# A two-layer graph network on one core: y and the norm's numbers get a place per graph, the weights land in other tiles and in another order

## The chip, the cores and the metric

The kernel runs on one core of a Trainium2 chip. The metric is the device time of one execution in microseconds. TensorE (PE) multiplies, VectorE (DVE), ScalarE (ACT) and GpSimd (POOL) do the element-wise work, and SyncE (SP) issues every DMA. Each engine works through its own queue in order and waits at semaphores for the others.

## The reference

128 graphs of 128 nodes with 384 features pass two attention layers with 12 heads of 32, each with a residual and a layer norm:

```python
# layer 0
q, k, v = x @ Wq.T, x @ Wk.T, x @ Wv.T + bv
scores = q @ k.T * 384**-0.5 + (adj + adj)      # per head
p = softmax(scores)                              # rows of zeros give 0
x = layernorm(x + (p @ v) @ Wo.T + bo)
# layer 1
q, k, v = x @ Wq + bq, x @ Wk + bk, x @ Wv + bv
scores = where(adj > 0, q @ k.T / sqrt(32) + beta * adj, -9e15)
x = layernorm(x + softmax(scores) @ v)
```

## The kernel before

The graphs go in 64 pairs (graph 0 and 1 of a pair). The projections of layer 0 and 1 and the output product of layer 0 take three TensorE products for each one of float32: a tile is split into a high part (ACT) and a low part (DVE or POOL), and hi·hi, hi·lo and lo·hi are added (`split_product`, L371 to L373). So each of the seven weight matrices is loaded once into a staging place (`w_stage`), copied to `w_hi` by ACT (L511) and `w_lo` is subtracted by DVE (L658) or POOL (L849).

A software pipeline written out by hand sets the order. Each engine has a `body(r, off)` that names its steps for pair n and for pairs up to four back (m1 to m4) or one ahead (p1). Bodies for n = -1 to 6 stand unrolled, then a loop of two bodies a turn runs 28 times, and eleven more bodies drain the pipeline. A helper does nothing where its pair does not exist. The queues of the engines are in that written order, so a step that waits holds everything behind it on its engine.

A graph of layer 0 passes: `scores` (PE, L421), `negate` (DVE, L699: negated scores and row minimum), `exps` (ACT, L594), `fold_scores0` (POOL, L901 and L904), `abs_max` and `inverse_sums0` (DVE), `normalise0` (POOL, L919), `flip_probs` (DVE, L715: 32x32 transposes into the tile `flip0`), `spread_probs` (SP, four DMAs from `flip0` to `prob0T`), `attend` (PE, L437), `project_out0`, `add_residual0` (DVE, L667), `norm_stats_of` (DVE), `inverse_std` (POOL, L859 to L866) and `norm_apply0` (ACT, L573). Layer 1 ends with `attention_out1` (DVE, L765), `residual1` (POOL, L911), the same norm steps, `norm_apply1` (ACT, L579) and `store` (SP, L265). `flip0` is also the scratch of `fold_scores0`, which therefore waits until the DMAs out of it have landed.

There is one tile `y[layer]` and one set of `stats`, `mean_var`, `var_eps`, `rstd` and `shift` for each layer. So `add_residual0` of a graph waits for `norm_apply0` of the graph before (`x1_done`), and `attention_out1` waits for the store of the graph before (`stored`).

Staging places are tiles that are otherwise used later: WV0 and WQ0 lie in `stage`, WK0 in `neg_s1`, WO0 in `prob1`, WQ1 in `prob1T`, WK1 in `prob0T`, WV1 in `prob0`. In the body of the first pair (`is_peeled`) the first writer of each such tile waits for the `w_lo` of the matrix in it: `exps` of layer 0 for WV1, `spread_probs` of layer 0 for WK1. POOL makes the low parts of WO0, WQ1, WK1 and WV1 at the end of its body -1, ahead of its body 0.

Four PSUM banks (`r_bank`) serve as a ring for the tiles in `RING_USERS`, each in the bank of its index modulo 4; the other four hold scores.

Of the kernel before, what the change touches and what calls it, by code (L numbers as in the profile page):

```python
# [53 lines left out]
RING_USERS = ["pv0_0", "ot_0", "g1_0", "v0_1", "g1_1", "v1_0", "g1_2", "pv1_1",  # L54
              "xt0", "wo_0", "v1_1", "xt1", "ot_1", "pv0_1", "g1_3", "g0_0",
              "g1_4", "g0_1", "g0_2", "wo_1", "g0_3", "g0_4", "g1_5", "g0_5",
              "pv1_0", "x1t0", "x1t1", "v0_0"]
# [54 lines left out]
def build(nc, x, adj, wts, bv0, bo0, bq1, bk1, bv1, beta, out):  # L112

    with ExitStack() as ctx:
# [9 lines left out]
        def sems(name, n=2):  # L124
# [30 lines left out]
        neg_max = [sb(f"neg_max{l}", [P, H]) for l in range(2)]  # L155
        prob = [sb(f"prob{l}", [P, H, N]) for l in range(2)]
        row_sum = [sb(f"row_sum{l}", [P, H]) for l in range(2)]
        inv_sum0 = sb("inv_sum0", [P, H])
        inv_sum1 = [sb(f"inv_sum1_{g}", [P, H]) for g in range(2)]
        inv_raw0 = sb("inv_raw0", [P, H])  # L160
        sum_neg0 = sb("sum_neg0", [P, H])
        abs_max0 = sb("abs_max0", [P, H])
# [5 lines left out]
        flat = [stage[:, 0:C * D], stage[:, C * D:NS * C * D]] + [t.rearrange("p a b -> p (a b)")[:, 0:C * D] for t in (  # L168
            neg_s[1][:], prob[1][:], probT[1][:].rearrange("p i h b -> p i (h b)"),
            probT[0][:].rearrange("p i h b -> p i (h b)"), prob[0][:])]  # L170
# [3 lines left out]
        y = [sb(f"y{l}", [P, D]) for l in range(2)]  # L174
        stats = [sb(f"stats{l}", [P, 6]) for l in range(2)]
        mean_var = [sb(f"mean_var{l}", [P, 2]) for l in range(2)]
        var_eps = [sb(f"var_eps{l}", [P, 1]) for l in range(2)]
        rstd = [sb(f"rstd{l}", [P, 1]) for l in range(2)]
        shift = [sb(f"shift{l}", [P, 1]) for l in range(2)]
# [14 lines left out]
        stored = sem("stored")  # L194
        w_hi_done = sem("w_hi_done")
# [40 lines left out]
        def _(sp):  # L236
# [25 lines left out]
            def store(q, g):  # L262
                if q.valid():
                    sp.wait_ge(x2_done, q.count(1, g, 1))
                    sp.dma_start(out[bass.ds(2 * q.index() + g, 1)].rearrange("g (j a) d -> a j (g d)", j=NB), y[1][:]  # L265
                                 ).then_inc(stored, 16)
# [61 lines left out]
            sp.wait_ge(stored, 16 * NG)  # L328
# [3 lines left out]
        def _(pe):  # L332
# [174 lines left out]
        def _(act):  # L507
            def high_weights(*which):
                for i in which:
                    act.wait_ge(w_loaded[i], 16)  # L510
                    act.activation(w_hi[i][:], w_stage[i], ACT.Copy).then_inc(w_hi_done, 1)  # L511
# [56 lines left out]
            def norm_apply0(q, g):  # L568
                if q.valid():
# [29 lines left out]
            def body(r, off):  # L599
# [17 lines left out]
                high_xT(p1, 1)  # L617
                exps(1, m3, 1, 0, 2)
# [357 lines left out]
```

## Time and profile before

| | us |
|---|---|
| median of 3 runs (2166.12 to 2169.29) | 2168.59 |
| the profiled execution | 2169.0 |
| its span, first to last instruction | 2167.2 |
| PE busy in it | 2072.6 |

All of the numbers below are of that one profiled execution; 1.8 us of its time lie outside the span. The page's slices show the fill (some 100 us) and the drain (some 130 us) with PE partly idle, and between them 9 tenths or more in every slice. A busy PE means that matmuls were in flight; their ends are modelled.

### The profile page before, as it was taken

To read this page: it belongs to the slowest core of one execution; us is meant where nothing else is said; L and a number is where in the kernel's file an instruction comes from. 1 tells how busy PE (TensorE), PEld (TensorE's weight loads), DVE (VectorE), ACT (ScalarE), POOL (GpSimd) and SP (SyncE) were. 2 spreads that over 40 slices of the span, in tenths; PEclk is the share of its full clock that TensorE was granted. 3 is DMA by queue.
4 is the path that set the end of the run, shared out by engine and by line. 5 is a ranking of instruction groups with operands and counts; after the bars stand their busy time and mean duration, and the time that the engine had idled before them with its cause. 6 is when DMAs were issued, how large, how long until landed. Compare 5 with 4: busy or idle time off the path is not lost.

```text
span 2167.2 us, 86729 instructions
## 1 busy us (share of the span) xinstructions
PE 2072.6 (96%) x23808; PEld 1911.8 (88%) x23808; DVE 1858.4 (86%) x8451; ACT 1835.6 (85%) x7688; POOL 1517.4 (70%) x2060
## 2 busy tenths in 40 slices
PE   5899999999999999999999999999999999999974
PEld 4799999999999999999999999999999999999963
DVE  2588898998898898898898898899899899889874
ACT  4489889888888888888988888988888988888874
POOL 3567777777777777777777777777777777777752
PEclk8899999999999999999999999999999999999986
DMA  4255565555565555565555556556556556555544
GB/s 127 62 132 143 136 155 145 135 152 138 137 153 137 137 153 139 134 153 141 139 146 149 132 145 151 136 140 154 135 139 152 144 136 152 139 137 151 132 120 107
DMA packets 234778, 300.33 MB, mean 139 GB/s; under 512 B 26704, under 2 KB 226384, under 8 KB 234576
## 3 DMA queue, kind: packets, MB, share of 16 engines
q1 hardware_dynamic: 234576, 298.43, 55.0%
q14 instruction: 172, 1.41, 0.2%
q8 instruction: 30, 0.49, 0.1%
HBM read 46.67 MB, written 25.17 MB: 33 GB/s over the span
## 4 chain that ended last, share of the span: by engine, by line
PE 73%; DVE 11%; issue 9%; POOL 3%; DMA 1%; DVEq 1%; SPq 1%; ACT 1%; POOLq 0%; ACTq 0%
PE r_bank L371 18%; PE r_bank L373 17%; PE r_bank L372 17%; PE s_bank L421 9%; PE r_bank L437 7%; DVE neg_s L699 5%; PE r_bank L354 2%; PE r_bank L449 2%; DVE x1T_lo L721 1%; DMA prob0T<-flip 1%; DVE neg_max L699 1%; DVE flip L715 1%; PE r_bank L364 1%; DVE v L776 1%; DVE sum_neg L748 1%
## 5 line engine op out<-in xcount | busy, mean ns | idle before, releaser
L594 ACT ACTIVATE prob<-neg_s,neg_max 128x128 f32<-128x128 f32 x3072 | 1190.4, 394 | 97.8 <-DVE flip L715 81.2
L594 ACT ACTIVATION_READ_ACCUMULATOR prob<-neg_s,neg_max 128x1 f32 x3072 | 593.1, 193 | 0.0
L919 POOL TENSOR_TENSOR prob<-prob,inv_sum 128x512 f32<-128x512 f32 x384 | 388.9, 1041 | 257.3 <-DVE inv_sum L787 257.3
L699 DVE CUSTOM_DVE_ANT_0 neg_s<-s_bank,bias 128x128 f32<-128x128 f32 x1536 | 334.7, 285 | 67.3 <-PE s_bank L421 63.7
L371 PE MATMUL r_bank<-xT_hi,w_hi 128*128 128x256 f32 x1152 | 329.2, 286 | 20.8 <-DVE xT_lo L721 19.3
L371 PE MATMUL r_bank<-x1T_hi,w_hi 128*128 128x256 f32 x1152 | 338.2, 294 | 6.7 <-DVE x1T_lo L721 3.3
L699 DVE CUSTOM_DVE_ANT_0 neg_s<-s_bank,adj 128x128 f32<-128x128 f32 x1536 | 333.4, 285 | 3.4 <-issue 2.8
L373 PE MATMUL r_bank<-xT_hi,w_lo 128*128 128x256 f32 x1152 | 328.0, 285 | 0.0
L372 PE MATMUL r_bank<-xT_lo,w_hi 128*128 128x256 f32 x1152 | 327.9, 285 | 0.0
L373 PE MATMUL r_bank<-x1T_hi,w_lo 128*128 128x256 f32 x1152 | 326.3, 283 | 0.0
L372 PE MATMUL r_bank<-x1T_lo,w_hi 128*128 128x256 f32 x1152 | 325.6, 283 | 0.0
L901 POOL TENSOR_TENSOR flip<-neg_s 128x768 f32<-128x768 f32 x128 | 234.6, 1832 | 102.2 <-DMA prob0T<-flip 100.0
L699 DVE DVE_READ_ACCUMULATOR2_ANT neg_max<- 128x1 f32 x3072 | 254.7, 83 | 0.0
L371 PEld LDWEIGHTS r_bank<-xT_hi,w_hi 128*128 128x128 f32 x1152 | 220.8, 192 | 22.6 <-DVE xT_lo L721 19.8
L371 PEld LDWEIGHTS r_bank<-x1T_hi,w_hi 128*128 128x128 f32 x1152 | 218.2, 189 | 25.5 <-issue 12.6
L715 DVE STREAM_TRANSPOSE flip<-prob 128x1536 f32<-128x1536 f32 x128 | 227.3, 1776 | 10.6 <-POOL prob L919 2.6
L715 DVE STREAM_TRANSPOSE stage<-prob 128x1536 f32<-128x1536 f32 x128 | 226.8, 1772 | 1.8 <-DMA prob1T<-stage 1.8
L373 PEld LDWEIGHTS r_bank<-xT_hi,w_lo 128*128 128x128 f32 x1152 | 221.0, 192 | 0.0
L372 PEld LDWEIGHTS r_bank<-xT_lo,w_hi 128*128 128x128 f32 x1152 | 220.8, 192 | 0.0
L372 PEld LDWEIGHTS r_bank<-x1T_lo,w_hi 128*128 128x128 f32 x1152 | 218.9, 190 | 0.0
L373 PEld LDWEIGHTS r_bank<-x1T_hi,w_lo 128*128 128x128 f32 x1152 | 218.6, 190 | 0.0
L776 DVE TENSOR_TENSOR v<-r_bank,bv_row 128x384 f32<-128x384 f32 x256 | 139.4, 545 | 45.1 <-issue 34.2
(82 smaller groups left out, 5332.0 us busy)
## 6 DMA issues: line engine op xcount, KB each, us to landing
prob0T<-flip SPq DMA_DIRECT2D x512, 192.0 KB, 3.5
prob1T<-stage SPq DMA_DIRECT2D x512, 192.0 KB, 3.6
x_in<-in_x_dram SPq DMA_DIRECT2D x128, 192.0 KB, 3.6
x_late<-x SPq DMA_DIRECT2D x64, 384.0 KB, 4.2
out_dram<-y SPq DMA_DIRECT2D x128, 192.0 KB, 2.4
adj<-in_adj_dram SPq DMA_DIRECT2D x256, 64.0 KB, 2.4
stage<-in_L_gnn_Wv_dram SPq DMA_DIRECT2D x1, 576.0 KB, 5.8
stage<-in_L_gnn_Wq_dram SPq DMA_DIRECT2D x1, 576.0 KB, 6.7
```

The costliest lines, as they stand in the source:

```text
L354: mm = pe.transpose(ring(f"xt{g}")[:, c * P:(c + 1) * P], x_in[q.parity][:, g, c * P:(c + 1) * P], ident[:])
L371: pe.matmul(dst, a_hi(c), b_hi(c), start=(c == 0), stop=False)
L372: pe.matmul(dst, a_hi(c), b_lo(c), start=False, stop=False)
L373: mm = pe.matmul(dst, a_lo(c), b_hi(c), start=False, stop=(c == C - 1))
L421: mm = pe.matmul(s_bank[j][:, c * N:(c + 1) * N], qT[layer][q.parity][rows, c, m], kT[layer][q.parity][rows, c, m], start=True, stop=True)
L437: mm = pe.matmul(ring(name)[HD * j:HD * (j + 1), c * N:(c + 1) * N], v[layer][q.parity][:, g, f], probT[layer][:, :, HC * c + j, :], start ...
L594: act.activation(prob[layer][:, h, :], neg_s[layer][:, h, :], ACT.Exp, bias=neg_max[layer][:, h:h + 1], scale=-1.0, accum_out=row_sum[laye ...
L699: dve.tensor_tensor_reduce(neg_s[layer][:, h, :], s_bank[b][:, (h // HC) * N:(h // HC + 1) * N], (adj0, bias1)[layer][q.parity][:, g, :], ...
L715: dve.transpose(flip[layer].rearrange("p (j h b) -> p h j b", j=NB, h=H), prob[layer][:].rearrange("p h (j a) -> p h j a", j=NB)).then_inc ...
L776: dve.tensor_tensor(v[layer][q.parity][:, g, :], ring(f"v{layer}_{g}")[:, 0:D], bv_row[layer][:], ALU.add).then_inc(v_out[layer], 1)
L901: pool.tensor_tensor(fold_a, neg_s[0][:, :, 0:N // 2], neg_s[0][:, :, N // 2:N], ALU.add).then_inc(fold_steps, 1)
L919: pool.tensor_tensor(prob[0][:, hs, :], prob[0][:, hs, :], inv_sum0[:, hs].unsqueeze(2).to_broadcast([P, HC, N]), ALU.mult).then_inc(probn ...
```

## The change

1. `y` and the norm's numbers exist for each layer and graph of a pair. The waits for the previous graph become waits for the same graph of the previous pair; `stored` is split in two semaphores.
2. The weights are loaded in the order WQ0, WK0, WV0, WO0, WQ1, WK1, WV1 and lie in: WV0 and WO0 in `stage`, WQ0 in `prob0`, WK0 in `prob0T`, WQ1 in `neg_s1`, WK1 in `prob1`, WV1 in `prob1T`. The waits for `w_lo` at the first pair name these. `w_hi_done` becomes one semaphore for each matrix.
3. WO0 is split in the middle of body -1, its low part by DVE instead of POOL. POOL makes the low parts of WQ1, WK1 and WV1 at the end of body 0.
4. `project_v` waits for the low part of its input (`lo_done`), which it did not before.
5. `RING_USERS` is rotated by nine places; as 28 is a multiple of 4, that renames the banks (each index one lower, modulo 4) and leaves which tiles share one.
6. Ten small tiles of 12 columns become slices of one tile `heads`. With it the start of `prob0`, `prob1`, `flip0`, `prob0T` and `prob1T` in SBUF moves from byte 128 of a 256-byte block to byte 224; the tiles `y` start at byte 224 too.

```diff
-RING_USERS = ["pv0_0", "ot_0", "g1_0", "v0_1", "g1_1", "v1_0", "g1_2", "pv1_1",
+RING_USERS = ["wo_0", "v1_1", "xt1", "ot_1", "pv0_1", "g1_3", "g0_0", "g1_4",
...
+        flat = [stage[:, 0:C * D], prob[0], probT_rows[0], stage[:, C * D:NS * C * D], neg_s[1], prob[1], probT_rows[1]]
...
+        y = [[sb(f"y{l}_{g}", [P, D]) for g in range(2)] for l in range(2)]
+        norm = [[sb(f"norm{l}_{g}", [P, 11]) for g in range(2)] for l in range(2)]
...
             load_x(Pair(0, 0))
-            load_weights(WV0)
             load_weights(WQ0)
+            load_weights(WK0)
             for layer, b_ in enumerate((bv0, bv1)):
                 sp.dma_start(bv_row[layer][:], b_.partition_broadcast(P)).then_inc(bv_loaded, 16)
-            load_weights(WK0)
+            load_weights(WV0)
...
-                        sp.wait_ge(w_lo_done[(WK1, WQ1)[layer]], 1)
+                        sp.wait_ge(w_lo_done[(WK0, WV1)[layer]], 1)
...
                     read[BANK[name]] = (v_out[layer], q.off, 1, g, 1)
+                    pe.wait_ge(lo_done[layer], q.count(1, g, 1))
...
-                            act.wait_ge(w_lo_done[(WV1, WO0)[layer]], 1)
+                            act.wait_ge(w_lo_done[(WQ0, WK1)[layer]], 1)
...
                 high_xT(p1, 1)
+                if is_peeled(r, off, -1):
+                    high_weights(WO0)
...
                 if is_peeled(r, off, -1):
-                    high_weights(WO0, WQ1, WK1, WV1)
-
-            high_weights(WV0, WQ0, WK0)
+                    high_weights(WQ1, WK1, WV1)
+
+            high_weights(WQ0, WK0, WV0)
...
-                    dve.wait_ge(x1_done, q.count(1, g, 0))
-                    dve.tensor_tensor(y[0][:], ring(f"wo_{g}")[:, 0:D], x_bo[q.parity][:, g, :], ALU.add
+                    dve.wait_ge(x1_done, q.plus(-1).count(1, g, 1))
+                    dve.tensor_tensor(y[0][g][:], ring(f"wo_{g}")[:, 0:D], x_bo[q.parity][:, g, :], ALU.add
...
-                    dve.wait_ge(stored, q.count(16, g, 0))
+                    dve.wait_ge(stored[g], q.plus(-1).count(8, 1, 8))
...
                 low_xT(p1, 1)
+                if is_peeled(r, off, -1):
+                    low_weights(WO0)
...
                 fold_scores0(n, 1)
-                if is_peeled(r, off, -1):
-                    low_weights(WO0, WQ1, WK1, WV1)
+                if is_peeled(r, off, 0):
+                    low_weights(WQ1, WK1, WV1)
```

POOL's queue from its first wait on, before; `w_lo3` to `w_lo6` are the low parts of WO0, WQ1, WK1 and WV1, `flip0` rows are `fold_scores0`, `prob0` rows `normalise0`:

```order
L849 TENSOR_TENSOR w_lo3<-prob1,w_hi3 128x1152
L849 TENSOR_TENSOR w_lo4<-prob1T,w_hi4 128x1152
L849 TENSOR_TENSOR w_lo5<-prob0T,w_hi5 128x1152
L849 TENSOR_TENSOR w_lo6<-prob0,w_hi6 128x1152
L901 TENSOR_TENSOR flip0<-neg_s0 128x768
L904 TENSOR_TENSOR flip0<-flip0 128x384
L919 TENSOR_TENSOR prob0<-prob0,inv_sum0 128x512 x3
L878 TENSOR_TENSOR x_bo0<-x_in0,bo_row 128x384 x2
L901 TENSOR_TENSOR flip0<-neg_s0 128x768
L904 TENSOR_TENSOR flip0<-flip0 128x384
L919 TENSOR_TENSOR prob0<-prob0,inv_sum0 128x512 x3
```

And after:

```order
L901 TENSOR_TENSOR flip0<-neg_s0 128x768
L904 TENSOR_TENSOR flip0<-flip0 128x384
L919 TENSOR_TENSOR prob0<-prob0,heads 128x512 x3
L878 TENSOR_TENSOR x_bo0<-x_in0,bo_row 128x384 x2
L901 TENSOR_TENSOR flip0<-neg_s0 128x768
L904 TENSOR_TENSOR flip0<-flip0 128x384
L849 TENSOR_TENSOR w_lo4<-neg_s1,w_hi4 128x1152
L849 TENSOR_TENSOR w_lo5<-prob1,w_hi5 128x1152
L849 TENSOR_TENSOR w_lo6<-prob1T,w_hi6 128x1152
L919 TENSOR_TENSOR prob0<-prob0,heads 128x512 x3
```

One of the four subtractions has left the queue; the other three stand between the fold and the normalisation of graph 1 of the first pair.

ACT's queue from its start, before (`w_hi` rows are the weights, `xT_hi` the first pair's input, `prob` rows its first `exps`):

```order
L511 ACTIVATE w_hi<-stage 128x1152 x2
L511 ACTIVATE w_hi<-neg_s 128x1152
L519 ACTIVATE xT_hi<-r_bank 128x3x128 x2
L554 ACTIVATE q0T<-r_bank 128x256 x3
L554 ACTIVATE k0T<-r_bank 128x256 x3
L511 ACTIVATE w_hi<-prob 128x1152
L511 ACTIVATE w_hi<-prob1T 128x1152
L511 ACTIVATE w_hi<-prob0T 128x1152
L511 ACTIVATE w_hi<-prob 128x1152
L594 ACTIVATE prob,row_sum<-neg_s,neg_max 128x128 x8
```

And after:

```order
L507 ACTIVATE w_hi<-prob 128x1152
L507 ACTIVATE w_hi<-prob0T 128x1152
L507 ACTIVATE w_hi<-stage 128x1152
L515 ACTIVATE xT_hi<-r_bank 128x3x128 x2
L507 ACTIVATE w_hi<-stage 128x1152
L550 ACTIVATE q0T<-r_bank 128x256 x3
L550 ACTIVATE k0T<-r_bank 128x256 x3
L507 ACTIVATE w_hi<-neg_s 128x1152
L507 ACTIVATE w_hi<-prob 128x1152
L507 ACTIVATE w_hi<-prob1T 128x1152
L590 ACTIVATE prob,heads<-neg_s,heads 128x128 x8
```

WO0 has moved ahead of the first q and k evictions; three matrices are left in front of the first `exps`.

## Rows read from the trace of the kernel before

**Rows 1.** The page: span, busy time of each engine.

```profile
span 2167.2 us, 86729 instructions
PE 2072.6 (96%) x23808; PEld 1911.8 (88%) x23808; DVE 1858.4 (86%) x8451; ACT 1835.6 (85%) x7688; POOL 1517.4 (70%) x2060
```

**Rows 2.** Windows: stretch, its length, busy (instructions) by engine, PE clock, DMA.

```profile
200.00:2000.00 1800.00, 1786.15 (x20744) 1651.13 (x20743) 1615.35 (x7362) 1588.72 (x6688) 1312.63 (x1788) 1.00 0.57 143
```

**Rows 3.** Waits within 200 to 2000: us in total, times, longest.

```profile
PE r_bank L437 <- DVE v L776: 9.2, 27, 0.4
PE r_bank L371 <- DVE x1T_lo L721: 3.3, 11, 0.4
...
DVE neg_s L699 <- PE s_bank L421: 53.8, 56, 1.7
...
DVE y L667 <- ACT x L573: 24.9, 55, 0.5
```

**Rows 4.** Timeline of the fill: start, duration, instruction [idle before <-releaser].

```profile
7.25 0.44 SPq L278 DMA_DIRECT2D prob<-in_L_gnn_Wo_dram  x1
...
16.01 0.55 PE L371 MATMUL r_bank<-xT_hi,w_hi 128*128 128x256 f32 x1 [9.94 <-DVE xT_lo L721]
...
26.33 2.67 POOL L849 TENSOR_TENSOR w_lo<-prob,w_hi 128x1152 fp32r<-128x1152 f32 x1 [9.31 <-ACT w_hi L511]
...
28.29 0.29 DVE L699 CUSTOM_DVE_ANT_0 neg_s<-s_bank,adj 128x128 f32<-128x128 f32 x1 [0.53 <-PE s_bank L421]
...
36.69 1.80 POOL L901 TENSOR_TENSOR flip<-neg_s 128x768 f32<-128x768 f32 x1
...
36.76 0.40 ACT L594 ACTIVATE prob<-neg_s,neg_max 128x128 f32<-128x128 f32 x1 [7.35 <-POOL w_lo L849]
...
42.20 0.55 PE L371 MATMUL r_bank<-xT_hi,w_hi 128*128 128x256 f32 x1 [9.34 <-DVE xT_lo L721]
...
54.37 1.82 POOL L901 TENSOR_TENSOR flip<-neg_s 128x768 f32<-128x768 f32 x1 [6.17 <-DMA prob0T<-flip]
...
56.27 1.01 POOL L904 TENSOR_TENSOR flip<-flip 128x384 f32<-128x384 f32 x1
...
58.59 3.04 POOL L919 TENSOR_TENSOR prob<-prob,inv_sum 128x512 f32<-128x512 f32 x3 [1.31 <-DVE inv_sum L787]
...
63.48 0.40 ACT L594 ACTIVATE prob<-neg_s,neg_max 128x128 f32<-128x128 f32 x1 [6.75 <-DVE flip L715]
```

**Rows 5.** DMA issues: tile, size, median us from issue to landing.

```profile
prob<-in_L_gnn_Wo_dram SPq DMA_DIRECT2D x1, 576.0 KB, 7.9
...
prob0T<-flip SPq DMA_DIRECT2D x512, 192.0 KB, 3.5
```

**Rows 6.** Timeline of PE in the steady part.

```profile
1035.66 0.28 PE L373 MATMUL r_bank<-x1T_hi,w_lo 128*128 128x256 f32 x1
1035.78 0.28 PE L371 MATMUL r_bank<-xT_hi,w_hi 128*128 128x256 f32 x1
...
1058.37 0.28 PE L373 MATMUL r_bank<-x1T_hi,w_lo 128*128 128x256 f32 x1
1058.57 0.64 PE L437 MATMUL r_bank<-prob1T,v 128*32 128x128 f32 x16
```

**Rows 7.** Timeline of the drain.

```profile
2103.87 0.56 DVE L667 TENSOR_TENSOR y<-r_bank,x_bo 128x384 f32<-128x384 f32 x1 [2.33 <-ACT x L573]
...
2104.02 0.39 ACT L594 ACTIVATE prob<-neg_s,neg_max 128x128 f32<-128x128 f32 x1
...
2105.28 0.52 DVE L677 BATCH_NORM_STATS2 stats<-y 128x6 f32<-128x384 f32 x1
...
2106.34 0.21 POOL L859 TENSOR_SCALAR var_eps<-mean_var 128x1 f32<-128x1 f32 x1 [3.48 <-DVE mean_var L680]
...
2110.57 3.00 SPq L306 DMA_DIRECT2D prob1T<-stage  x4
...
2151.76 0.56 DVE L765 TENSOR_TENSOR y<-r_bank,inv_sum 128x384 f32<-128x384 f32 x1 [1.12 <-DMA out_dram<-y]
```

More of the change, by code:

```diff
@@ L154, in build @@
         neg_s = [sb(f"neg_s{l}", [P, H, N]) for l in range(2)]
-        neg_max = [sb(f"neg_max{l}", [P, H]) for l in range(2)]
+        heads = sb("heads", [P, 10 * H])
+        per_head = [heads[:, i * H:(i + 1) * H] for i in range(10)]
+        neg_max, row_sum, inv_sum1 = per_head[0:2], per_head[2:4], per_head[4:6]
+        inv_sum0, inv_raw0, sum_neg0, abs_max0 = per_head[6:10]
         prob = [sb(f"prob{l}", [P, H, N]) for l in range(2)]
[L157 to L162, printed above, removed]
         flip0 = sb("flip0", [P, H * N])
@@ L167, in build @@
         probT = [sb(f"prob{l}T", [P, NB, H, HD]) for l in range(2)]
-        flat = [stage[:, 0:C * D], stage[:, C * D:NS * C * D]] + [t.rearrange("p a b -> p (a b)")[:, 0:C * D] for t in (
-            neg_s[1][:], prob[1][:], probT[1][:].rearrange("p i h b -> p i (h b)"),
-            probT[0][:].rearrange("p i h b -> p i (h b)"), prob[0][:])]
+        probT_rows = [t[:].rearrange("p i h b -> p i (h b)") for t in probT]
+        flat = [stage[:, 0:C * D], prob[0], probT_rows[0], stage[:, C * D:NS * C * D], neg_s[1], prob[1], probT_rows[1]]
+        flat = [t if i in (WV0, WO0) else t[:].rearrange("p a b -> p (a b)")[:, 0:C * D] for i, t in enumerate(flat)]
         w_stage = [t.rearrange("p (c o) -> p c o", c=C) for t in flat]
@@ L173, in build @@
         o1T = sb("o1T", [P, C, N])
[L174 to L179, printed above, removed]
+        y = [[sb(f"y{l}_{g}", [P, D]) for g in range(2)] for l in range(2)]
+        norm = [[sb(f"norm{l}_{g}", [P, 11]) for g in range(2)] for l in range(2)]
+        stats, mean_var, var_eps, rstd, shift = ([[t[:, a:b] for t in n] for n in norm] for a, b in ((0, 6), (6, 8), (8, 9), (9, 10), (10, 11)))
         mask1 = sb("mask1", [P, N])
@@ L264, in store @@
                     sp.wait_ge(x2_done, q.count(1, g, 1))
[L265 to L266 removed]
+                    sp.dma_start(out[bass.ds(2 * q.index() + g, 1)].rearrange("g (j a) d -> a j (g d)", j=NB), y[1][g][:]
+                                 ).then_inc(stored[g], 16)
             def keep_x1(q):
@@ L326, in _ @@
             iterations(sp, body)
-            sp.wait_ge(stored, 16 * NG)
+            for g in range(2):
+                sp.wait_ge(stored[g], 8 * NG)
         @block.tensor
@@ L510, in high_weights @@
                     act.wait_ge(w_loaded[i], 16)
-                    act.activation(w_hi[i][:], w_stage[i], ACT.Copy).then_inc(w_hi_done, 1)
+                    act.activation(w_hi[i][:], w_stage[i], ACT.Copy).then_inc(w_hi_done[i], 1)
             def high_xT(q, g):
@@ L578, in norm_apply1 @@
                     act.wait_ge(rstd_steps[1], q.count(3, g, 3))
-                    act.activation(y[1][:], y[1][:], ACT.Identity, bias=shift[1][:], scale=rstd[1][:]
+                    act.activation(y[1][g][:], y[1][g][:], ACT.Identity, bias=shift[1][g][:], scale=rstd[1][g][:]
                                    ).then_inc(x2_done, 1)
@@ L692, in negate @@
                                 if is_peeled(q.r, q.off, 0):
-                                    dve.wait_ge(w_lo_done[WK0], 1)
+                                    dve.wait_ge(w_lo_done[WQ1], 1)
                                 dve.wait_ge(bias1_steps, q.count(3, g, 3))
@@ L712, in flip_probs @@
                             dve.wait_ge(w_lo_done[WV0], 1)
-                            dve.wait_ge(w_lo_done[WQ0], 1)
+                            dve.wait_ge(w_lo_done[WO0], 1)
                     dve.wait_ge(probT_loaded[layer], q.count(16 * NB, g, 0))
@@ L830, in body @@
                 low_x1T(m1, 0)
-            low_weights(WV0, WQ0, WK0)
+            low_weights(WQ0, WK0, WV0)
             iterations(dve, body)
```

38 lines of the change are left out of this document (19 added, 19 removed).

## The prediction

> **What bounds the kernel now.** I read the page first, then the windows by stage, then the waits of the steady part, and last the timelines of the fill and the drain. The page says that PE is busy for 2072.6 of 2167.2 us [rows 1], so some 95 us without PE are all that better covered waits could win. The window from 200 to 2000 shows where they are not: PE is idle there for 1800 - 1786.15 = 13.9 us in all, at the full clock [rows 2]. So about 81 of the 95 us lie in the fill and the drain, and each part of the change has to be read there apart from the 56 steady pairs.
>
> In the steady part the waits of PE itself come to 9.2 + 3.3 = 12.5 us [rows 3], all for DVE: 27 times (once a loop turn) for the tile v, 11 times for the low part of x1. The wait that the change takes away is another: DVE waits 55 times for ACT's norm result before it writes y, 24.9 us in all, or 0.45 us a pair. The reader is to see what comes after it on DVE: the layer-1 scores, for which DVE waits 56 times, 53.8 us in all, 0.96 us a pair [rows 3].
>
> In the fill the timeline tells a clear story [rows 4]. DVE has the first negated scores from 28.3 us on, but ACT's first exponential starts at 36.76 after 7.35 us of waiting for POOL's low weights: its output tile still holds WV1. POOL makes four of these from 26.33 to 36.69, 2.59 us each, and only then folds. PE stands for 9.34 us until 42.20 because of that. From there the chain goes round: fold, normalise, flip, DMA out of the flip tile, next fold. The second fold at 54.37 waited for the DMA, its second half starts at 56.27 and ends at 57.28, and graph 1 is normalised from 58.59; ACT had waited 6.75 us for the flip that follows.
>
> **The change part by part.**
>
> *The first exponentials.* After the change they wait for WQ0's low part, made before PE's first projection at 16.01. ACT then has three `w_hi` left in front of them instead of four and would be done by about 28.3; the first row minimum is there at about 28.6. I take 28.7 for the first exponential: 36.76 - 28.7 = 8.0 us earlier. POOL's first fold needs all twelve heads, which DVE gives 0.21 us apart, so it starts near 31.1 instead of 36.69 and ends near 34.0; the sums need the last exponential, 8.0 us earlier than before, at about 34.1. So the fold is no bound, and normalise, flip, DMA and the next fold all move by 8.0 us: that fold starts at 54.37 - 8.0 = 46.4 and ends at 49.3.
>
> *The subtractions are still to be done.* Three of them now stand behind this fold: 3 x 2.59 = 7.8 us, to 57.05. Graph 1's normalisation is behind them in POOL's queue and could have started at 58.59 - 8.0 = 50.6. It starts at 57.05. Of the 8.0 us there remain 58.59 - 57.05 = 1.5 us. Behind it wait DVE's flip, the exponentials of the next pair (the row at 63.48), through them the split of the input of the pair after, and PE. PE's gap of 9.34 us before 42.20 goes, and nearly as long a one comes back ten to twenty microseconds later. The chain of folds and DMAs then repeats as before, 1.5 us earlier, until PE is the bound from about 90 us on. I take -1.5 us. The bounds: 0 if the shorter gap at 42 and the longer one behind it leave PE at its lower clock for longer, and -8.0 if the three subtractions were hidden.
>
> *WO0 and the order of loads.* WQ0 and WK0 come first and WV0 third; but PE's first projection waits for the split of x, and that stands behind all three on ACT and on DVE, so 16.01 stays. WO0 is issued at 7.25 and lands 7.9 us later [rows 4, 5], at 15.2; ACT and DVE split it in a good microsecond each, ACT before PE has finished the first group of nine products begun at 16.01, DVE in a gap that lasts until the first v. Cost nothing; if WO0 landed two microseconds later, ACT would hold the first q by about one, which the same chain would carry: bound +1.
>
> *A place for each graph in the steady part.* DVE's wait of 0.45 us goes, all it does until the layer-1 scores comes 0.45 us earlier, and there it waits 0.96 + 0.45 us. Those scores are PE's, and PE waits for nothing that this stretch of DVE makes: its 12.5 us hang on work behind the scores, in the start of the next body. The norm's result gets earlier too, but ACT's queue is not what PE waits for. I take 0, with -12.5 us as the far end if all of PE's waits went.
>
> *The extra wait in `project_v`.* Four groups a pair, 256 in all, carry one more semaphore that has always been reached. What it costs PE is bounded by two group starts [rows 6]: a q or k group, which has two such waits, starts 0.12 us after the product before it, the same step as inside a group (1035.66 to 1035.78), so a second wait is hidden behind a 256-column product. An `attend` group with three waits starts 0.20 us after (1058.37 to 1058.57), 0.08 more. `project_v` will have two, thus nearer to the first: 0. The far end is 256 x 0.08 = 20 us.
>
> *The drain.* DVE's write of y of the last graph of layer 0 waits 2.33 us for ACT [rows 7]; that goes. Behind it stand the statistics of layer 1, the sum of the last exponentials (ended at 2104.02 + 0.39 = 2104.4) and then the statistics at 2105.28, which can now start 0.2 us after the sum, at 2104.6. POOL had idled 3.48 us for them, and behind it are ACT's norm, a store and the DMAs at 2110.57, which the rest of the drain needs. So -0.7 us. The wait of 1.12 us for a store before the write at 2151.76 goes too, but the other graph's flip, DMA and product end later than that branch: 0. The bounds are 0 and -2.3.
>
> *Banks and slices.* The rotation gives each tile the same neighbours in the ring, and slices of one tile need no more instructions: 0.
>
> The DMAs between `flip0` and `prob0T` take 3.5 us from issue to landing [rows 5], with rows of 1536 bytes that start at byte 128 of a 256-byte block, and will start at byte 224. The Trainium skill (DMA: Bandwidth & Descriptors, How a descriptor splits into AXI transactions) states that a first transaction that starts inside such a block still costs the beats from the block's start. By it a row goes from 52 to 55 beats of 32 bytes, so a transfer would take at most 6% longer, 0.2 us, which an estimate from that page would put on some six transfers of the fill and drain: +1.2 us. No row here shows two alignments of one transfer, so the sum leaves it out.
>
> *The sum.* -1.5 - 0.7 = -2.2 us on an execution of 2169.0 us gives 2166.8. The median of the runs is 0.4 us below that execution, so I predict 2166.5 us.
>
> **The rivals.** What this kernel's measurement can tell from no change is about 0.2%, 4.3 us.
>
> *A, the forecast*: 2166.5, the fill's gain is handed back at the three subtractions. Its own range is 2164.3 to 2169.5.
>
> *B, the fill's gain stays.* If POOL's subtractions were covered, 8.0 + 0.7 us would go: 2159.9. For it speaks that POOL idles 6.17 us before the fold at 54.37; against it, that this idle time is ahead of the fold and the subtractions are behind it in an ordered queue. 7%.
>
> *C, the steady part follows.* DVE's 0.45 us reach PE, and the 12.5 us of PE's waits go: 2168.6 - 2.2 - 12.5 = 2154; a third of it would already be told from no change. For it speaks that DVE is 90% busy there and that PE's waits are all for DVE; against it, the 0.96 us for which DVE waits in between in every pair. 12%.
>
> *D, slower: the new waits on PE's own queue.* PE is the bound for 1800 us, so whatever its queue loses is lost. The place is the start of the 256 v groups; at the attend's price it costs 20 us, 2166.5 + 20 = 2186.5. It decides from (4.3 + 2.2) / 256 = 0.025 us a group on. For it speaks that the attend rows show a price at all; against it, the q and k rows. 12%.
>
> **How the numbers follow.** A has 69%, B 7%, C 12%, D 12%. Part of C is too small to be told, so faster by over 0.2% has 0.17, slower by over 0.2% 0.12, and within it 0.71. For 8 in 10 the range reaches down to B, 2160, and up into the lower part of D, 2172.
>
> **What would show it.** Right in the fill: ACT's first exponential at 28.7 without a wait for POOL, the three `w_lo` rows on POOL from 49.3 to 57.05, the normalisation behind them at 57.05, and PE's gap of 9.3 us gone at 34 and another near 50 to 66. Right in the steady part: no DVE wait for ACT's x at L667's successor, about 1.4 us a pair for the scores, and PE's idle time from 200 to 2000 still near 14 us. Wrong if the steady pairs take another time than before, if q starts later than 18 us, or if a v group stands more than 0.12 us behind its predecessor.

## The result and the profile after

The changed kernel takes 2171.66 us in the median of 22 runs (2168.26 to 2173.96), the kernel before 2168.55 in 22 runs beside it: a ratio of 1.0014 with a 95% interval of 1.0007 to 1.0020. It is slower by about 3 us, where 2 us faster was forecast. That is inside the range, but on the other side of no change.

The page of the changed kernel: its span and busy times, against [rows 1].

```profile
span 2171.1 us, 86842 instructions
PE 2073.2 (95%) x23808; PEld 1909.7 (88%) x23808; DVE 1865.2 (86%) x8452; ACT 1834.6 (85%) x7688; POOL 1515.3 (70%) x2059
```

PE does the same 23808 products in 0.6 us more. The fill comes next, from the timeline of after, against [rows 4] (start, duration, instruction, idle before).

```profile
28.62 0.40 ACT L590 ACTIVATE prob<-neg_s,heads 128x128 f32<-128x128 f32 x1 [0.34 <-DVE heads L697]
...
34.06 0.36 PE L366 MATMUL r_bank<-xT_hi,w_hi 128*128 128x256 f32 x1 [1.28 <-DVE xT_lo L719]
...
46.21 1.81 POOL L901 TENSOR_TENSOR flip<-neg_s 128x768 f32<-128x768 f32 x1 [6.13 <-DMA prob0T<-flip]
...
49.06 2.66 POOL L849 TENSOR_TENSOR w_lo<-neg_s,w_hi 128x1152 fp32r<-128x1152 f32 x1
...
54.24 2.65 POOL L849 TENSOR_TENSOR w_lo<-prob1T,w_hi 128x1152 fp32r<-128x1152 f32 x1
...
54.84 0.90 PE L349 MATMUL r_bank<-ident,x_in 128*128 128x128 f32 x3 [3.95 <-DVE o0T_lo L719]
...
56.84 3.04 POOL L919 TENSOR_TENSOR prob<-prob,heads 128x512 f32<-128x512 f32 x3
...
61.73 0.40 ACT L590 ACTIVATE prob<-neg_s,heads 128x128 f32<-128x128 f32 x1 [12.06 <-DVE flip L713]
...
62.20 0.90 PE L349 MATMUL r_bank<-ident,x_in 128*128 128x128 f32 x3 [3.72 <-DVE v L774]
```

The reader sees the predicted chain to within 0.3 us: the first exponential at 28.6, the fold at 46.2, three subtractions behind it, the normalisation at 56.8 and the next pair's exponentials 1.75 us earlier than before. PE's gap of 9.34 us has become 1.28 us, ACT's wait before 61.73 has grown from 6.75 to 12.06 us, and PE now waits 3.95 and 3.72 us near 54 and 62, where one gap of about nine was forecast. Up to here the change gains what was forecast.

The steady part, 200 to 2000, first by windows (after, against [rows 2]), then by waits (after, against [rows 3]: us in total, times, longest).

```profile
200.00:2000.00 1800.00, 1780.76 (x20673) 1645.17 (x20672) 1611.70 (x7344) 1583.64 (x6668) 1309.49 (x1781) 1.00 0.58 142
```

```profile
DVE neg_s L697 <- PE s_bank L417: 66.0, 56, 1.2
...
DVE v L774 <- issue: 30.6, 27, 1.3
...
DVE y L665 <- PE r_bank L368: 10.4, 48, 0.3
PE r_bank L366 <- DVE x1T_lo L719: 9.6, 27, 0.6
PE r_bank L433 <- DVE v L774: 9.5, 27, 0.4
```

PE's idle time has grown from 13.9 to 19.2 us, and one row accounts for the growth: it now waits for the low part of x1 in every loop turn (9.6 us, 27 times; before 3.3 us, 11 times). DVE's wait for ACT's x is gone, as predicted; a part of it has become a wait for PE's product (10.4 us, 48 times). The row that explains PE's wait is `v <- issue`: idle time of DVE in which no semaphore holds it. The same view of the kernel before has it too, and the prediction's rows leave it out:

```profile
DVE v L776 <- issue: 22.9, 27, 1.0
```

27 times is once a turn. The timelines of DVE at the end of the same loop turn show where; before, and then after.

```profile
1081.62 0.55 DVE L721 TENSOR_TENSOR x1T_lo<-r_bank,x1T_hi 128x384 fp32r<-128x384 f32 x1
1083.10 0.56 DVE L776 TENSOR_TENSOR v<-r_bank,bv_row 128x384 f32<-128x384 f32 x1 [0.93 <-issue]
1083.58 0.55 DVE L721 TENSOR_TENSOR x1T_lo<-r_bank,x1T_hi 128x384 fp32r<-128x384 f32 x1
```

```profile
1084.91 0.55 DVE L719 TENSOR_TENSOR x1T_lo<-r_bank,x1T_hi 128x384 fp32r<-128x384 f32 x1
1086.64 0.56 DVE L774 TENSOR_TENSOR v<-r_bank,bv_row 128x384 f32<-128x384 f32 x1 [1.17 <-issue]
1087.12 0.55 DVE L719 TENSOR_TENSOR x1T_lo<-r_bank,x1T_hi 128x384 fp32r<-128x384 f32 x1
```

The first row is the last step of a turn, the second the first step of the next: the gap is the loop's back edge. The records of the trace that no view counts as busy hold the branch too. From DVE's branch to the first instruction of the next turn it takes 1.30 us in the median before and 1.51 us after. ScalarE needs 0.19 us for the same, GpSimd 0.225 us and PE 0.28 us. The second `x1T_lo` of the turn is what PE waits for. A turn (two pairs; mean of PE's 27 intervals from branch to branch) takes 64.519 us before and 64.745 us after: 27 x 0.226 = 6.1 us.

The drain, from the timeline of after, against [rows 7].

```profile
2107.99 0.56 DVE L665 TENSOR_TENSOR y<-r_bank,x_bo 128x384 f32<-128x384 f32 x1 [2.00 <-PE r_bank L368]
...
2110.47 0.21 POOL L859 TENSOR_SCALAR norm<-norm 128x1 f32<-128x1 f32 x1 [3.35 <-DVE norm L678]
...
2114.69 2.95 SPq L300 DMA_DIRECT2D prob1T<-stage  x4
```

DVE's wait of 2.33 us for ACT has become one of 2.00 us for PE. From that write to the DMAs it is 2114.69 - 2107.99 = 6.70 us, before 2110.57 - 2103.87 = 6.70 us: nothing was gained there.

By stages, after against before: from PE's first scores to its first loop branch 279.6 against 279.1 us (+0.5), the loop +6.1, from its last branch to the end 116.4 against 119.0 us (-2.6), and -0.1 ahead of the first scores. That is the 3.9 us by which the spans differ. So two things were to be explained: the longer turn, and a fill that was 1.9 us ahead of the kernel before at about 120 us (by DVE's writes of v) and had lost it by 306.

### The profile page after: what moved, and what is told of

Read it like the earlier page. It is cut to its first block, busy times and chain, and to the rows that moved or that the text cites. A ratio compares the mean times of both kernels' runs of the same rounds, so it can differ in the third digit from the quotient of the medians.

```text
span 2171.1 us, 86842 instructions
## 1 busy us (share of the span) xinstructions
PE 2073.2 (95%) x23808; PEld 1909.7 (88%) x23808; DVE 1865.2 (86%) x8452; ACT 1834.6 (85%) x7688; POOL 1515.3 (70%) x2059
## 4 chain that ended last, share of the span: by engine, by line
PE 69%; DVE 12%; issue 9%; POOL 4%; DMA 3%; SPq 1%; DVEq 1%; ACT 0%; POOLq 0%
PE r_bank L366 17%; PE r_bank L367 16%; PE r_bank L368 16%; PE s_bank L417 8%; PE r_bank L433 6%; DVE neg_s L697 4%; DMA prob0T<-flip 3%; PE r_bank L349 2%; PE r_bank L445 2%; DVE flip L713 2%; DVE heads L697 1%; DVE x1T_lo L719 1%; SPq L300 1%; POOL flip L901 1%; PE r_bank L359 1%
## 5 line engine op out<-in xcount | busy, mean ns | idle before, releaser
L590 ACT ACTIVATE prob<-neg_s,heads 128x128 f32<-128x128 f32 x3072 | 1190.0, 392 | 104.9 <-DVE flip L713 96.6
L590 ACT ACTIVATION_READ_ACCUMULATOR prob<-neg_s,heads 128x1 f32 x3072 | 588.6, 192 | 0.0
L919 POOL TENSOR_TENSOR prob<-prob,heads 128x512 f32<-128x512 f32 x384 | 388.9, 1041 | 242.2 <-DVE heads L785 242.2
L697 DVE DVE_READ_ACCUMULATOR2_ANT heads<- 128x1 f32 x3072 | 256.2, 83 | 0.1
L713 DVE STREAM_TRANSPOSE flip<-prob 128x1536 f32<-128x1536 f32 x128 | 227.5, 1777 | 13.7 <-POOL prob L919 6.1
```

The costliest lines, as they stand in the source:

```text
L590: act.activation(prob[layer][:, h, :], neg_s[layer][:, h, :], ACT.Exp, bias=neg_max[layer][:, h:h + 1], scale=-1.0, accum_out=row_sum[laye ...
L697: dve.tensor_tensor_reduce(neg_s[layer][:, h, :], s_bank[b][:, (h // HC) * N:(h // HC + 1) * N], (adj0, bias1)[layer][q.parity][:, g, :], ...
L713: dve.transpose(flip[layer].rearrange("p (j h b) -> p h j b", j=NB, h=H), prob[layer][:].rearrange("p h (j a) -> p h j a", j=NB)).then_inc ...
L919: pool.tensor_tensor(prob[0][:, hs, :], prob[0][:, hs, :], inv_sum0[:, hs].unsqueeze(2).to_broadcast([P, HC, N]), ALU.mult).then_inc(probn ...
```

## The experiments

"Place" below is a count of DVE's instructions in the compiled program: those ahead of its loop, plus those in the loop, gives the place of its branch. The y split takes three of them out of the loop (444 to 441), since some waits and the register arithmetic for them fall away; the order of loads adds one ahead of it. Counted in the traces, DVE's records up to the next turn's first instruction agree with these places to within one. The times of stages in the table come from one profiled execution of each kernel, and kernels with the fill of before differ there by up to 1.8 us (279.1 to 280.9). Each ratio is to the kernel before, run on the same chip at the same time.

| kernel | ahead + loop = place | branch to next turn, us | turn, us | first scores to first branch, us | ratio (95% interval) |
|---|---|---|---|---|---|
| E1 y split | 1045+441=1486 | 1.55 | 64.752 | 278.4 | 1.0030 (1.0017, 1.0042) |
| after | 1046+441=1487 | 1.51 | 64.745 | 279.6 | 1.0014 (1.0007, 1.0020) |
| E8 y split, weights | 1046+441=1487 | 1.48 | 64.710 | 276.0 | 1.0009 (1.0000, 1.0019) |
| before | 1045+444=1489 | 1.30 | 64.519 | 279.1 | 1 |
| E2 start bytes | 1045+444=1489 | 1.27 | 64.519 | 279.8 | 1.0002 (0.9993, 1.0011) |
| E4 wait in project_v | 1045+444=1489 | 1.30 | 64.504 | 279.9 | 0.9985 (0.9976, 0.9994) |
| E3 weights | 1046+444=1490 | 1.21 | 64.429 | 276.4 | 0.9973 (0.9962, 0.9984) |
| E5 after, 3 in loop | 1046+444=1490 | 1.18 | 64.414 | 279.6 | 0.9973 (0.9963, 0.9983) |
| E6 after, 3 ahead | 1049+441=1490 | 1.20 | 64.413 | 279.3 | 0.9976 (0.9966, 0.9987) |
| E7 all but y split | 1046+444=1490 | 1.19 | 64.412 | 276.7 | 0.9980 (0.9971, 0.9989) |
| E9 old bytes, 3 | 1049+441=1490 | 1.18 | 64.385 | 275.1 | 0.9967 (0.9955, 0.9980) |
| E10 old bytes, 5 | 1051+441=1492 | 1.10 | 64.324 | 276.5 | 0.9958 (0.9943, 0.9973) |
| E11 old bytes, 9 | 1055+441=1496 | 0.84 | 64.085 | 276.7 | 0.9930 (0.9915, 0.9945) |
| F1 before, 11 | 1056+444=1500 | 0.56 | 63.869 | 279.9 | 0.9916 (0.9902, 0.9929) |
| E12 old bytes, 13 | 1059+441=1500 | 0.55 | 64.010 | 275.9 | 0.9929 (0.9914, 0.9944) |
| F2 old bytes, 17 | 1063+441=1504 | 0.53 | 64.466 | 277.1 | 0.9975 (0.9964, 0.9986) |
| F4 before, 23 | 1068+444=1512 | 0.53 | 63.918 | 280.9 | 0.9936 (0.9922, 0.9949) |
| F3 old bytes, 25 | 1071+441=1512 | 0.26 | 63.520 | 279.5 | 0.9869 (0.9854, 0.9884) |
| F5 after, 25 | 1071+441=1512 | 0.26 | 63.532 | 279.7 | 0.9887 (0.9872, 0.9902) |
| F6 old bytes, 33 | 1079+441=1520 | 0.26 | 63.517 | 279.7 | 0.9880 (0.9865, 0.9895) |

### E1 to E4: one part of the change at a time

**E1**, part 1 alone on the kernel before.

```diff
-        y = [sb(f"y{l}", [P, D]) for l in range(2)]
+        y = [[sb(f"y{l}_{g}", [P, D]) for g in range(2)] for l in range(2)]
...
-                    dve.wait_ge(x1_done, q.count(1, g, 0))
+                    dve.wait_ge(x1_done, q.plus(-1).count(1, g, 1))
...
+        small = sb("small", [P, 8 * H + 44])
```

> The kernel before with only y and the norm's numbers per graph of a pair (the small tiles are packed behind them, so that prob, flip0 and probT keep their byte 128 of a 256-byte block). Theory S (the split itself costs): DVE reaches the loop's end 0.45 us a pair earlier in its work, and what it meets there is longer; the turn goes from 64.52 to about 64.74 us, PE waits for x1T_lo about 27 times in 200 to 2000 instead of 11, the time is 6 us above before less some 2 us of drain: about 2172. Theory A (start bytes of the tiles) and theory P (the added waits of project_v): the turn stays at 64.52, only the drain gets 2.6 us shorter as in the changed kernel, about 2166. In every theory the wait of DVE for ACT's x is gone.

Measured: 2174.77 us, somewhat more than theory S had. The waits of E1 from 200 to 2000:

```profile
DVE v L772 <- issue: 31.2, 27, 1.4
...
PE r_bank L367 <- DVE x1T_lo L717: 10.3, 27, 0.6
```

They are close to those of after. The turn is as long as after's, and 27 x 0.233 = 6.3 us is all that separates E1 from before. So the longer turn comes with the y split; theory S stands for now, and theories A and P are out for the turn.

**E2**, part 6 alone: the ten small tiles as slices of one, which moves five tiles to byte 224.

```diff
-        neg_max = [sb(f"neg_max{l}", [P, H]) for l in range(2)]
+        heads = sb("heads", [P, 10 * H])
```

> The kernel before with only the ten small tiles made slices of one, so that prob0, prob1, flip0, prob0T and prob1T start at byte 224 instead of 128 of a 256-byte block, with the same instructions in the same order. Theory A: the DMAs between flip0 and prob0T get slower (3.5 to 3.6 us), POOL's folds wait for them longer (about 99 instead of 64.5 us in 200 to 2000), and with the loop turn 0.2 us longer and 2 us more in the unrolled bodies the time is about 2175 to 2177. Theories S and P: nothing changes, 2168.5, at most 1 us more.

Measured: 2168.66 us, no difference, the turn the same. POOL's fold waits 24.0 us for the DMAs from 100 to 300, against 22.6 before; E1 and E4, with the old start bytes, have 23.1 and 23.4, so that is no clear difference either. Alone the part costs nothing that can be measured.

**E3**, parts 2 and 3 alone.

```diff
-                if is_peeled(r, off, -1):
-                    low_weights(WO0, WQ1, WK1, WV1)
+                if is_peeled(r, off, 0):
+                    low_weights(WQ1, WK1, WV1)
```

> The kernel before with only the other landing places, the other order of the weights and POOL's three subtractions moved behind the second fold. In all theories the turn is 64.52 as before. The fill as predicted: first exponential at 28.6, the normalisation behind the subtractions near 56.9, 1.5 to 1.9 us gained by 90 us: 2166.8. If the gain is lost again in the unrolled bodies by the weights' part itself (theory W: the shifted fill meets other waits until 306 us), 2168 to 2169.

Measured: 2162.53 us. The fill gains 2.7 us by the first branch, more than 1.5 to 1.9 (0.9 us of further gain stands ahead of the first scores), and keeps it; that the turn falls by 0.09 us (2.4 us in all) no theory had. DVE has one instruction more ahead of its loop here, and its branch takes 1.21 us.

**E4**, part 4 alone.

```diff
+                    pe.wait_ge(lo_done[layer], q.count(1, g, 1))
                     wi = (WV0, WV1)[layer]
```

> The kernel before with only project_v's wait for the low part of its input; PE's loop has 7 more instructions. Theory P: each of the 256 groups, or the loop's start on PE, costs something: 6.3 us over the 28 turns (0.225 us a turn, 0.028 us a group), in all about 7 us, 2175.6. Theories S and A: nothing, 2168.5.

Measured: 2165.70 us. Theory P is out. It is a little faster than before, which was not expected; the turn gives 0.4 us of it, the rest is in the drain of the profiled run, and it isn't explained.

The four parts add up to 6.3 + 0.2 - 5.9 - 2.7 = -2.1 us, while together they gave +3. So they interact. The branch times of the first rows of the table suggested a new theory, L: not what the y split does, but where DVE's code then lies.

### E5 and E6: three empty instructions in the changed kernel

**E5** puts three semaphore increments that nobody needs into the loop, **E6** the same three once ahead of it.

```diff
+                if not isinstance(r, int) and off == LOOP_FROM + 1:
+                    for _ in range(3):
+                        dve.sem_inc(dve_passed, 1)
                 values_out(0, n, 0)
```

```diff
+    if ahead:
+        ahead()
...
-            iterations(dve, body)
+            iterations(dve, body, ahead=lambda: [dve.sem_inc(dve_passed, 1) for _ in range(3)])
```

> The changed kernel with three semaphore increments more on DVE in each loop turn (ahead of the second body), so that DVE's loop has 444 instructions again as before, not 441. Measured so far: from DVE's branch at the loop's end to the first instruction of the next turn it takes 1.30 us before (turn 64.52), 1.55 with the y split alone (turn 64.75), 1.51 after (64.745), 1.21 with the weights alone (64.43). Theory L (where DVE's branch stands or how long its loop is sets that time): it falls to 1.2 to 1.3 us and the turn to 64.43 to 64.52, the time by 6 to 9 us to 2163 to 2166. Theory S (the split shifts DVE's work and waits, and the code has no part in it): three instructions more change nothing or cost a little: turn 64.75 or more, 2171.7 or more.

> The changed kernel with the three increments on DVE once, ahead of its loop: the loop keeps its 441 instructions, but its branch stands at the same count as in the kernel above (1049 + 441 = 1046 + 444 = 1490). Theory L1 (the place of the branch in DVE's code sets the time from the branch to the next turn): 1.2 to 1.3 us, turn 64.43 to 64.52, about 2163 to 2166, the same as the kernel above. Theory L2 (the loop's length sets it): 1.5 us stays, turn 64.74, 2171.7. Theory S: 2171.7 as well.

Measured: 2161.86 and 2162.72 us, 9 to 10 us less than the changed kernel's 2171.66 by adding work (8 to 9 us by the ratios), and a little less than L and L1 had. The waits of E6 from 200 to 2000:

```profile
DVE v L776 <- issue: 19.4, 27, 1.0
PE r_bank L435 <- DVE v L776: 9.5, 27, 0.4
PE r_bank L368 <- DVE x1T_lo L721: 0.9, 4, 0.3
```

PE's wait for `x1T_lo` falls from 9.6 to 0.9 us. Theory S is refuted, L2 (the loop's length) too, since E6 keeps 441 instructions; L1, the place of the branch, holds here.

### E7 and E8: how the parts interact

**E7** is the changed kernel with part 1 undone (and the old names of the banks), **E8** has parts 1 to 3 at the old start bytes; their edits are those of E1 to E4 put together.

> The changed kernel without the y split (one y and one set of the norm's numbers for each layer, as before): the weights, project_v's wait and the slices stay. If the parts add up: -5.9 (weights) -2.7 (wait) +0.2 (slices) on 2168.4 = 2160.0, the loop turn 64.43, the first branch of PE's loop at 302.4. If the weights' gain in the fill is lost by meeting the wait or the slices (start bytes), PE's first branch comes at 304 to 306 instead and the time is 2162 to 2165.

> The kernel before with the y split and the weights' part, tiles at their old start bytes, no added wait. If the parts add up: -5.9 + 6.3 = +0.4, 2168.8; PE's first loop branch at 302.4 - 1.0 = 301.4, and the turn 64.75 because DVE's loop has 441 instructions. If it is the split together with the weights that loses the fill's gain (after has its first branch at 306.57), the first branch comes at 305 to 306.5 and the time is about 2172 to 2173.

Measured: 2162.74 and 2170.33 us. Neither is what the parts add up to (2160.0 and 2168.8). PE's first branch stands 304.1 and 303.5 us behind the span's start, where the sums had 302.4 and 301.4; E7 thus meets its other forecast, that of a lost gain (304 to 306, 2162 to 2165), and E8 lies between its two. E7 has no y split and the same place as E5 and E6, which have it: turns of 64.412, 64.414 and 64.413 us. With the place held equal the split is worth 0 in the steady part. Counted from PE's first scores, which came late in these two executions (27.4 us, 27.0 before), the fill's gain is there at the first branch (276.7 and 276.0 us); in after, E5 and E6 it isn't (279.3 to 279.6). E7 lacks the split, E8 the start bytes. That suggested that it takes both to lose it. The times don't bear this out: E7 (0.9980) is no faster than E5 and E6 (0.9973 and 0.9976) at the same turn. DVE's wait for POOL's fold, from 100 to 300, in after, then in E8:

```profile
DVE heads L746 <- POOL flip L904: 9.7, 11, 2.0
```

```profile
DVE small L746 <- POOL flip L904: 3.6, 3, 1.6
```

Of the kernels so far, the three with both have 8.4 to 9.7 us here, E1, E2, E7 and E8 have 3.6 to 5.0.

### E9 to E12: old start bytes, and the place moved on

All four are the changed kernel with its tiles at the old start bytes and 3, 5, 9 or 13 increments ahead of DVE's loop.

```diff
-        heads = sb("heads", [P, 10 * H])
+        neg_max = [sb(f"neg_max{l}", [P, H]) for l in range(2)]
...
-            iterations(dve, body)
+            iterations(dve, body, ahead=lambda: [dve.sem_inc(dve_passed, 1) for _ in range(13)])
```

> The changed kernel with the tiles prob0, prob1, flip0, prob0T, prob1T and y back at byte 128 of a 256-byte block (neg_max as tiles of its own, the other small ones packed behind y) and three increments more on DVE ahead of its loop, its branch at 1049 + 441 = 1490. Theory A2 (the start bytes lengthen the DMAs out of flip0 a little, and only together with the y split, which brings DVE to the fold's result earlier, does it cost something, in the unrolled bodies): DVE's wait for POOL's fold between 100 and 300 goes from 8.4 to 9.7 (the three kernels with both) to 3.6 to 5, PE's first loop branch comes 276 to 277 us after its first scores instead of 279.5, the turn stays 64.41 and the time is 2158.5 to 2160. Theory W2 (three parts at once disturb the fill, whatever the bytes): first branch at 279.5, time 2162.5.

> As the kernel before in this list but with five increments: DVE's branch at 1492. From DVE's branch to the next turn's first instruction it took 1.55 us with the branch at 1486, 1.48 to 1.51 at 1487, 1.27 to 1.30 at 1489, 1.18 to 1.21 at 1490. Theory F (a floor is reached): 1.15 to 1.2, turn 64.41. Theory Q (it goes on falling by 0.05 to 0.1 us an instruction, until a block of code ends): 1.0 to 1.1, turn 64.2 to 64.3, some 3 us less time.

> Nine increments: DVE's branch at 1496. Theory F: 1.15 to 1.2 us, turn 64.41. Theory Q with a block of 8: back up to 1.3 to 1.55 us, turn 64.5 to 64.75; with a larger block: 0.7 to 0.9 us and a turn near 64.1.

> Thirteen increments: DVE's branch at 1500. Theory F: 1.15 to 1.2 us, turn 64.41. Theory Q with a block of 8: as at 1492; with a block of 16 or more and a steady fall: 0.4 to 0.7 us, turn 64.0 to 64.1, when PE's once-a-turn wait for v (9.4 us in 200 to 2000) would be gone.

Measured: 2160.25, 2157.73, 2152.12 and 2150.85 us. E9 has the fill's gain back (275.1 us, and 3.1 us of waits for the fold), as theory A2 says; E10 has the gain too, but waits of 5.8 us. By time alone E9 and E6 can't be told apart, since their intervals overlap; only the stage in the trace speaks for A2, and F5 below speaks against it. For the turn, theory F falls: the time from the branch goes down steadily, by (1.55 - 0.55) / 14 = 0.07 us for each instruction of place from 1486 to 1500.

### F1 to F3: the kernel before moved, and the end of the fall

**F1** is the kernel before with nothing but 11 increments ahead of DVE's loop; **F2** and **F3** go on from E12 with 17 and 25.

> The kernel before with nothing changed but eleven increments on DVE ahead of its loop: DVE's branch at 1056 + 444 = 1500, where the last kernel had 0.55 us from the branch to the next turn's first instruction. Theory L1 (the place of the branch in DVE's code alone): 0.5 to 0.6 us here too, the turn from 64.52 down to 64.0 to 64.1, 28 turns of it -12 to -14 us: 2154 to 2156. Theory S (the y split is needed for that): little changes, turn 64.4 or more, 2165 or more.

> As the kernel with 13 increments (1500: 0.55 us, turn 64.01), with 17: DVE's branch at 1504. A straight line through 1486 (1.55) and 1500 (0.55) gives 0.07 us an instruction, so 0.27 us at 1504, the turn no lower than 64.0, since PE is then nearly all of it; 2150 to 2151. If a block of code ends between 1500 and 1504 the time from the branch jumps to 1.3 us or more and the turn to 64.5 or more, about 2164.

> With 25 increments: DVE's branch at 1512. If blocks are 16 instructions long it is as at 1496 (0.84 us, turn 64.08, 2152); if 32 or more, one of two: still 0.2 to 0.3 us as for ScalarE and GpSimd (turn 64.0), or past a block's end, with 1.2 us or more (turn above 64.4).

Measured: 2150.25, 2162.45 and 2139.55 us. F1 shows by itself that the place alone moves the time: eleven empty instructions make the kernel before 18 us faster, and DVE's branch time is that of E12 at the same place. It is faster than L1 had (2154 to 2156), since the turn fell to 63.87 and not to 64.0. In F2 the branch is short (0.53 us), yet the turn is long again. Its waits from 200 to 2000:

```profile
DVE neg_s L700 <- issue: 16.6, 27, 0.8
PE r_bank L436 <- DVE v L777: 16.2, 28, 0.7
```

The stall has not gone, it has moved: 22 instructions behind the loop's start DVE stands for up to 0.8 us, ahead of the turn's first negated scores. In F3 neither stall is there. None of the theories had this.

### F4 to F6: both kernels at the good place

**F4** is the kernel before with 23 increments, **F5** the changed kernel with 25, nothing else edited, **F6** F3 with 33.

> The kernel before with 23 increments on DVE ahead of its loop, the branch at 1068 + 444 = 1512, where the kernel with the old start bytes and both parts of the change had 0.26 us from the branch to the next turn, a turn of 63.52 and 2139.5. Theory L1: the turn is 63.5 to 63.6 here too; the fill's gain (2 to 3 us) is missing: 2141 to 2143. Theory S2 (with the stall gone the y split is worth something in every turn, which it was not with the stall): the turn stays near the 63.87 that the kernel before had with 11 increments, about 2150.

> The changed kernel with nothing else edited but 25 increments on DVE ahead of its loop, its branch at 1071 + 441 = 1512. Theory L1: 0.26 us from branch to next turn, turn 63.5, so 27.5 x 1.2 us less than the changed kernel: 2139 to 2140; with the start bytes' 2 to 3 us in the unrolled bodies 2140 to 2142. If the start bytes cost in every turn once PE waits for nothing else, 63.6 or more and above 2143.

> Old start bytes, both parts, 33 increments: the branch at 1520. If the good stretch goes on: 0.26 us, turn 63.5, 2139.5. If code blocks are 32 instructions long, 1520 is to 1512 as 1488 to 1480, and at 1488 the branch took about 1.4 us: turn 64.6, about 2168.

Measured: 2153.47, 2142.14 and 2140.46 us. The windows of F5, and DVE at its back edge:

```profile
200.00:2000.00 1800.00, 1798.28 (x21032) 1673.68 (x21031) 1635.93 (x7460) 1611.06 (x6789) 1334.66 (x1811) 1.00 0.59 144
```

```profile
1070.18 0.55 DVE L721 TENSOR_TENSOR x1T_lo<-r_bank,x1T_hi 128x384 fp32r<-128x384 f32 x1
1070.77 0.56 DVE L776 TENSOR_TENSOR v<-r_bank,bv_row 128x384 f32<-128x384 f32 x1
```

PE is idle for 1.7 us of 1800, and the back edge has no gap.

F5 bears on theory A2 too. Up to its increments, at about 240 us, its program is that of after, start bytes and y split included. The 22nd of DVE's 256 writes of v shows how far each had come; before, after and F5:

```profile
218.91 0.52 DVE L776 TENSOR_TENSOR v<-r_bank,bv_row 128x384 f32<-128x384 f32 x1
```

```profile
219.97 0.52 DVE L774 TENSOR_TENSOR v<-r_bank,bv_row 128x384 f32<-128x384 f32 x1
```

```profile
217.01 0.52 DVE L776 TENSOR_TENSOR v<-r_bank,bv_row 128x384 f32<-128x384 f32 x1
```

F5 is 1.9 us ahead of the kernel before at a point where after is 1.1 us behind, and its wait for the fold from 100 to 300 is 3.9 us, not 8.4 to 9.7; F2 and F3, with the old start bytes, have 5.9 and 6.9 us. So the split and the start bytes together don't make a kernel lose the gain. Why after, E5 and E6 lost it is open, and no run here tells whether it varies from one execution or chip to the next.

F4 has its branch at the same place, 1512, but in its waits from 200 to 2000 the stall is somewhere else again:

```profile
DVE y L767 <- issue: 13.7, 28, 0.5
...
DVE stats L679 <- issue: 6.7, 27, 0.3
```

So the branch's place is not the whole law: F4 starts at 1068 with 444 instructions and stalls, F3 and F5 start at 1071 with 441 and don't, F6 at 1079 doesn't either. Whether the loop's start or its length decides between F4 and F5 wasn't tried. F5 and F6 came within a microsecond of their forecasts, F4's forecast of a turn of 63.5 was wrong.

The only starts of DVE's loop without a stall are the latest ones, 1071 and 1079 (0.26 us from branch to next turn). The other engines have short branches in every kernel: GpSimd with 161 or 162 instructions in its loop (0.225 us), ScalarE with 424 records a turn in the trace (0.19 us), and PE with about 870 besides its products (0.28 us). The Trainium skill (Runtime: NRT & Kernel Launch, Instruction fetch mechanics) gives a rule for this: most engines hold 512 instructions in two blocks of 256, PE four times as many, code is fetched ahead in sequence, and a taken branch whose target is not in the blocks held has to wait for a fetch. As an estimate from these figures, a loop of 441 fits into two blocks only if it starts within the first 71 instructions of one, and the block's boundary would lie between 1068 and 1071. The runs agree with that, but the boundary isn't seen by itself, and the rule doesn't say why the stall shrinks evenly from 1486 to 1500 or moves into the loop at 1504.

## Why the prediction was wrong, point by point

- **What bounds the kernel.** PE does, as said. The reading of the waits failed: it took `DVE neg_s <- PE` as the next thing behind the wait removed and passed over `v <- issue`, 22.9 us in 27 waits, the cause of both of PE's rows in [rows 3]: in F5, without the gap at the back edge, PE is idle for 1.7 us and not 13.9. The 1.3 us at each back edge was the number of the steady part that the edit moved.
- **A place for each graph in the steady part, 0.** This is the step that failed. Its own mechanism was right: the wait is gone, DVE now waits 66.0 / 56 = 1.18 us a pair for the layer-1 scores (1.4 forecast) and some 0.2 us a pair for PE's product before it, and E5 to E7 give 0 with the place held. What it left out is that the edit takes three instructions out of DVE's loop. E1 gives that +0.233 us a turn, 6.3 us, which three empty instructions undo.
- **The fill, -1.5.** The chain came as worked out to 0.3 us. Alone (E3) it is -2.7 us at the first branch. In the changed kernel it was +0.5 at the first branch: 1.9 us ahead at 120 us, and lost between 130 and 240 us. What took it is open; the y split together with the start bytes was the theory, but F5 has both and is still 1.9 us ahead at 217 us.
- **The start bytes.** They were left out of the sum, rightly as far as the runs show: alone they cost nothing that can be measured (E2: 1.0002, 0.9993 to 1.0011). The medians from issue to landing are 3.6 us in after and 3.5 before, but E9 with the old start bytes has 3.6 too. The Trainium skill (DMA: Bandwidth & Descriptors, How a descriptor splits into AXI transactions), from which the prediction's estimate of 1.2 us came, is thus neither confirmed nor refuted here.
- **WO0 and the order of loads, 0.** PE's first projection starts at 15.97 us (16.01 before). But the order adds one instruction ahead of DVE's loop, which in E3 shortens the turn by 0.09 us.
- **The extra wait in `project_v`, 0, and rival D.** Right: E4 isn't slower.
- **The drain, -0.7.** Wrong at the place named, where the wait only changed its releaser. The stage is 2.6 us shorter, but kernels without the split differ there by as much (115.9 us in E7, 118.4 in E3, 119.5 in F4, 119.0 before), so it can't be put down to any part.
- **The rivals.** None of them is what happened. B named the fill's gain, C the steady part, D the wrong queue: the slower side came from DVE's code and not from PE's waits.

## What to carry to other kernels

Before an edit is priced, count what it does to each engine's code ahead of and inside the loop, and look in the waits for a row `<- issue` that comes once a turn at the first step of the loop: that engine stands at its back edge, and its price moves with the place of the code. An A/B test of any edit in such a kernel measures the shift too; hold the place equal with empty instructions, or first find a place without the stall. Here 25 of them ahead of the loop took the changed kernel from 1.0014 to 0.9887 of the kernel before (F5), some 27 us, nine times the change under test. F3, with the old start bytes as well, is the fastest version (2139.55 us).

## What the runs showed that was not expected

- From DVE's branch to the next turn's first instruction it took 0.26 to 1.55 us, with the same work in the loop; from place 1486 to 1500 0.07 us less for each instruction. Why it falls so evenly isn't settled. It would fit a fetch that starts at a fixed place in the code, so that a branch further behind it finds the fetch more advanced.
- The stall doesn't end with the branch: at 1496 a small part of it stood ahead of the layer-1 scores (5.6 us in 27 waits), at 1504 it stood 22 instructions behind the loop's start (16.6 us in 27 waits), in F4 at three steps (13.7, 6.7 and 5.0 us).
- At place 1500 the turn is 63.87 us with the kernel before (F1) and 64.01 with both parts (E12), though the branch times are equal. This is open.
- In F3, F5 and F6 PE has one gap of 1.7 to 2.3 us near 246 us, outside the loop, so a shift moves stalls of the unrolled bodies too; it takes back what the fill had gained (first branch at 279.5 to 279.7 us).
